# First attention of a fused eight-stage kernel: a searched order of steps, heads' score pieces in turn, a tie step on one tensor, fewer row copies

## What is computed

```python
qkv = layernorm(x) @ w_attn.T + b_attn          # split into q, k, v by head
att = einsum('bhid,bhjd->bhij', q, k) / sqrt(8) # causal
S = relu(att[:, 0]); S[..., 0] = 0; S *= 1 - eye(T)
FF = cumsum(shift_down_one_row(S), axis=1)      # a penalty for each (i, j)
att = att - FF[:, None]
rank = rank of FF within its row (ties: lower j first)
keep = (rank < min(budget - 1, i + 1)) | eye(T) # budget = int(0.2 * 2048) = 409
y = softmax(where(keep, att, -inf)) @ v
x = x + y @ w_proj.T + b_proj
```

## Time and profile before

| | us |
|---|---|
| median of three runs | 2910.46 (2904.49 to 2914.45) |
| the profiled execution | 2907.81 |
| its span in the profile | 2906.0 |
| before the search | 0 to 97 |
| search | 97 to 307 |
| attention | 307 to 926 |
| stages 2 to 8 | 926 to 2906 |
| busy over the span: TensorE, VectorE, ScalarE, GpSimd | 88%, 62%, 62%, 12% |

### The profile page before, as it was taken

One profiled execution on the slowest core, in us unless ns is written; L12 is line 12 of the kernel. 1 busy time (PEld: TensorE's weight loads), 2 busy tenths in 40 slices (PEclk: granted clock), 3 DMA queues, 4 the chain that ended last, 5 costly groups with the idle time before them and its releaser, 6 DMA issues. The chain is left out here.

```text
span 2906.0 us, 73996 instructions
## 1 busy us (share of the span) xinstructions
PE 2553.9 (88%) x30564; PEld 1586.3 (55%) x30564; DVE 1802.5 (62%) x5184; ACT 1796.3 (62%) x3222; POOL 347.1 (12%) x718
## 2 busy tenths in 40 slices
PE   7989788888888999999997999999999999886586
PEld 3668466665665532122113657667667676564355
DVE  6899788777875651000005577787787778653852
ACT  3799565555665269999993266666667667421331
POOL 3100332222220100000000100000000000034025
PEclk8989799999999999999998999999999999897698
DMA  3410001111002011100000000000000000312103
GB/s 118 71 26 2 7 12 17 17 17 17 17 10 55 1 59 54 56 1 1 1 1 17 28 14 8 8 2 7 7 2 8 8 2 2 98 23 40 29 19 55
DMA packets 85111, 68.12 MB, mean 23 GB/s; under 512 B 40776, under 2 KB 73688, under 8 KB 84392
## 3 DMA queue, kind: packets, MB, share of 16 engines
q1 hardware_dynamic: 76328, 57.09, 8.2%
q0 software_dynamic: 8448, 6.30, 1.7%
HBM read 47.21 MB, written 19.96 MB: 23 GB/s over the span
## 5 line engine op out<-in xcount | busy, mean ns | idle before, releaser
L1890 ACT ACTIVATE arena<-ps 128x1024 f32<-128x1024 f32 x512 | 474.1, 1281 | 25.9 <-PE ps L1840 24.0
L1341 DVE CUSTOM_DVE_ANT_0 arena<-ps,arena 128x1024 f32<-128x1024 f32 (+7 forms) x384 | 349.9, 931 | 107.0 <-PE ps L1217 91.1
L2268 DVE CUSTOM_DVE_ANT_0 arena<-ps,arena 128x512 f32<-128x512 f32 (+3 forms) x640 | 371.1, 643 | 26.6 <-PE ps L2132 25.8
L1293 ACT ACTIVATE arena<-ps 128x1024 f32<-128x1024 f32 (+3 forms) x320 | 275.2, 896 | 130.6 <-PE ps L1250 127.0
L2225 ACT ACTIVATE arena<-arena 128x1152 f32<-128x1152 f32 (+15 forms) x256 | 306.4, 1199 | 63.1 <-DVE arena L2268 63.1
L2132 PE MATMUL ps<-arena 64*128 64x512 f32 (+3 forms) x1280 | 270.3, 547 | 3.5 <-ACT arena L2201 1.1
L1851 PE MATMUL ps<-arena 128*32 128x512 f32 x2048 | 273.0, 604 | 0.0
L2163 PE MATMUL ps<-arena 128*64 128x128 f32 x4352 | 262.3, 275 | 0.0
L2163 PEld LDWEIGHTS ps<-arena 128*64 128x64 f32 x4352 | 235.3, 137 | 33.4 <-issue 28.7
L2187 ACT COPY arena<-ps 128x512 f32<-128x512 f32 (+3 forms) x410 | 189.7, 517 | 76.0 <-PE ps L2149 73.7
L1245 PE MATMUL ps<-arena 64*128 64x64 f32 x4352 | 217.0, 232 | 20.4 <-ACT arena L1293 12.2
(11 more groups left out here) (312 smaller groups left out, 4003.9 us busy)
## 6 DMA issues: line engine op xcount, KB each, us to landing
arena<-scr_q SPq DMA_DIRECT2D x256, 32.0 KB
scr_s<-scr_f SPq DMA_DIRECT2D x1, 4096.0 KB, 16.8
arena<-scr_k SPq DMA_DIRECT2D x32, 128.0 KB
arena<-by_head_k SPq DMA_DIRECT2D x16, 192.0 KB
arena<-scr_s SPq DMA_DIRECT2D x16, 192.0 KB, 2.7
arena<-by_head_q SPq DMA_DIRECT2D x28, 96.0 KB
by_head_k<-arena SPq DMA_DIRECT2D x5, 512.0 KB, 4.5
scr_x<-arena SPq DMA_DIRECT2D x2, 1024.0 KB, 5.4
```

What stands on the lines that cost most here:

```text
L1293: e.activation(turned_block(u, kc), src, ACT.Exp, scale=-1.0).then_inc(exped, 1)
L1341: e.tensor_tensor_reduce(scored_block(u, g)[:, lo:hi], PS[:, 1024 * (k % 2):1024 * (k % 2) + hi - lo], NF[t][:, lo:hi], -1.0, mxs[:, col - ...
L1890: e.activation(PTR[k % RS], PS[:, at(n):at(n) + 1024], ACT.Sigmoid, scale=float(1 / np.sqrt(8.0))).then_inc(weighed, 1)
L2268: e.tensor_tensor_reduce(slot(u, t, g)[:, lo:hi], PS[:, base(step) + 512 * g:base(step) + 512 * g + hi - lo], bias, -1.0, mxs[:, col - 1:c ...
```

## The change

- Row copies: q rows of the c-th group of four tiles are copied only to row groups 1 to c, and k rows of chunk c only to row group c: 9 copies instead of 24. They count on the three semaphores `d_q`, one per group, and a matmul waits only for the copies of its own four tiles.
- Pieces: the list of score pieces runs (piece 0 of both heads), (piece 1 of both heads). A second piece waits for its own head's first piece, by number.
- Ties: step 4 was (count > allowed) x (is a tie), reading two tensors; it is now (count > allowed) x -2^-126 by a tensor_scalar that reads the count alone. Step 5 is now (penalty - threshold) > that: at a tie the difference is zero, which is above -2^-126 and not above 0. The two tensors change places in steps 5 and 6.
- Order: `TileOrder` becomes a search. A `Course` is a partial order with its clocks. From each of up to 30 courses every candidate that could start within 0.5 us of the earliest one is tried; of the courses that reach the same counts of steps the one with the least idle time stays (TensorE's idle time counts double), and of all, the 30 with the least. Each instruction has two times: what it takes of its engine and when its result arrives. A change between matmuls of 64 and of 128 rows costs 0.115. GpSimd's split and the blocking by scans are followed; a shift may come at most two units past the last close; a divide is put behind the step that copies its last sums.

Nothing else is changed: the same units, the same instructions per unit, the same banks and extras. The diff, cut to its core:

```diff
+TINY = float(2.0 ** -126)
...
+    def on_tensor(self, rows, ready, lasts, ends):
+        start = self.tensor + (0.115 if self.rows not in (None, rows) else 0.0)
+        if ready > start:
+            self.idle += 2 * (ready - start)
+            start = ready
+        self.rows, self.tensor = rows, start + lasts
+        return start + ends
...
+    BLOCKS = {"turn": ((0.19, 0.34), (0.37, 0.54), (0.55, 0.73), (0.73, 0.91)),
+              "exp": ((0.29, 0.38), (0.5, 0.6), (0.71, 0.81), (0.92, 1.02)),
+              "pv": ((0.11, 0.39), (0.22, 0.4), (0.33, 0.61), (0.44, 0.62))}
...
+        self.pieces = [(u, g, i) for u in range(self.n) for i in range((units[u][0] + 8) // 8) for g in range(2)]
+        self.turns = [(u, kc) for u in range(self.n) for kc in range((units[u][0] + 4) // 4)]
+        self.last = [(t + 4) // 4 - 1 for t, _ in units]
+        self.last_of = {t: u for u, (t, _) in enumerate(units)}
+        courses, best = [Course()], None
+        while courses:
+            reached = {}
+            for c in courses:
+                options = [(max(c.tensor + (0.115 if c.rows not in (None, rows) else 0.0), ready), kind) for kind, rows, ready in self.candidates(c)]
+                if not options and (best is None or c.vector < best.vector):
+                    best = c
+                for start, kind in options:
+                    if start <= min(options)[0] + 0.5:
+                        x = c.copy()
+                        self.go_on(x, kind)
+                        key = (*x.at.values(), len(x.flips), len(x.adds))
+                        if key not in reached or x.idle < reached[key].idle:
+                            reached[key] = x
+            courses = sorted(reached.values(), key=lambda c: c.idle)[:width]
...
-        pieces = [(u, g, i) for u in range(n) for g in range(2) for i in range((units[u][0] + 8) // 8)]
...
-            options = sorted((max(now["pe"] + (0.2 if m != mode[0] else 0.0), ready) + bias.get(kind, 0.0), kind, m) for kind, m, ready in candidates())
...
+    def may_shift(self, c):
+        w = c.at["shift"]
+        if w < min(self.n, c.at["close"] + 3) and (w < 2 or (w - 2, self.last[w - 2]) in c.turned):
+            return self.split_at(c, w)
+        return None
+
+    def candidates(self, c):
+        free = min(c.free) + 0.05
+        if c.at["score"] < len(self.pieces):
+            u, g, i = self.pieces[c.at["score"]]
+            over = self.over(self.scored, u)
+            if u < c.at["shift"] + 4 and (over is None or over in c.turned):
+                yield "score", 64, c.biased[-2] + 0.06 if len(c.biased) >= 2 else 0.0
+        if c.at["turn"] < len(self.turns):
+            u, kc = self.turns[c.at["turn"]]
+            over = self.over(self.turned, u)
+            if u in c.copied and (over is None or over in c.summed):
+                yield "turn", 64, max(c.copied[u] + 0.06, free)
+        v = c.at["close"]
+        kept_back = v >= 1 and self.held(c, v - 1)
+        if v < self.n and (v, self.last[v]) in c.exped and not kept_back:
+            yield "close", 128, max(free, c.exped[v, self.last[v]] - 0.44 * self.last[v] - 0.03)
+        if v == self.n and v - 1 not in c.merged and not kept_back:
+            yield "merge", 128, max(free, c.kept[v - 1] + 0.05)
+        ready = self.may_shift(c)
+        if ready is not None:
+            yield "shift", 128, max(free, ready + 0.06)
+        if c.flips:
+            yield "flip", 128, max(free, c.flips[0][1] + 0.06)
+        if c.adds:
+            yield "add", 128, max(free, c.adds[0][1] + 0.05)
...
+                if x[0] >= 3 and j == 3:
+                    c.scans = c.scans[-2:] + ((c.vector, c.vector + 0.267 * nb),)
...
+        if kind == "close":
+            v = c.at["close"]
+            c.at["close"] += 1
+            use = (s, ("close", v))
+            if v:
+                self.merge(c, v - 1, max(free, c.kept[v - 1] + 0.05), use)
+            w, ready = c.at["shift"], self.may_shift(c)
+            with_shift = ready is not None and ready < c.tensor + 0.2 + 0.055 * (self.units[v][0] + 1)
+            for kc in range(self.last[v] + 1):
+                if with_shift and w not in c.shifted and kc == (self.last[v] + 2) // 2:
+                    self.shift(c, w, ready + 0.06, (None, ("close", v)), 1)
+                end = c.summed[v, kc] = c.on_tensor(128, max(free, c.exped[v, kc] + 0.05), *self.BLOCKS["pv"][self.blocks(v, kc) - 1])
+                c.emit("pv", v, kc, use=use if v == 0 and kc == 0 else None)
...
+        if c.ended and not c.flips and not c.adds and self.last_of[c.ended[0]] in c.taken:
+            t, c.ended = c.ended[0], c.ended[1:]
+            end = c.on_vector(c.taken[self.last_of[t]] + 0.05, 0.49, 0.56)
+            c.emit("divide", t)
+            c.flips += ((t, end),)
+            c.divided += (t,)
...
                 e.dma_start(XB, a["L0_attn_a_b_proj"].unsqueeze(0).to_broadcast([128, 128])).then_inc(d_late, 16)
-                for c in range(4):
-                    for by, ready, of, to in ((filled, 7 + c, q_rows, q_rows), (qkv_biased, 3 * c + 3, k_t, k_rows)):
-                        w.wait_ge(by, ready)
-                        for g in range(1, 4):
-                            e.dma_start(cols(to, c)[32 * g:32 * g + 8, :], cols(of, c)[0:8, :]).then_inc(d_rows, 16)
+                for c in range(1, 4):
+                    w.wait_ge(filled, 7 + c)
+                    for g in range(1, c + 1):
+                        e.dma_start(cols(q_rows, c)[32 * g:32 * g + 8, :], cols(q_rows, c)[0:8, :]).then_inc(d_q[c - 1], 16)
+                    w.wait_ge(qkv_biased, 3 * c + 3)
+                    e.dma_start(cols(k_rows, c)[32 * c:32 * c + 8, :], cols(k_t, c)[0:8, :]).then_inc(d_q[c - 1], 16)
                 rpe_sync(e, w)
                 for i in range(3):
                     w.wait_ge(part, 2 * i + 1)
@@ -740,7 +837,6 @@
 
 
             q_rows, k_rows = reg(D0 + 13312, 2048), reg(D0 + 15360, 2048)
-            d_rows = sem("f_d_rows")
 
             def head_rows(g):
 
@@ -760,7 +856,7 @@
                             w.wait_ge(f_relu, n - 3)
                         g = c0 // 512
                         if g:
-                            w.wait_ge(d_rows, 384)
+                            w.wait_ge(d_q[t // 4 - 1], 16 * (t // 4 + 1))
                         q, k = head_rows(g)
                         e.matmul(bank(n % 4, c1 - c0), q[:, 128 * t:128 * t + 128], k[:, c0:c1], start=True, stop=True).then_inc(f_scores, 1)
                     else:
@@ -1083,7 +1179,7 @@
                 for i, x in enumerate(steps):
                     first = ahead if k == 1 else 0
                     extras.setdefault((16 * (k - 1) + first + (15 - first) * i // len(steps), 1, 0), []).append(x)
-            plan = TileOrder(units, tiles, extras, space, {"score": -0.3, "shift": 0.1, "flip": -0.65, "add": -0.8, "turn": -0.15, "close": -0.3})
+            plan = TileOrder(units, tiles, extras, space, 30)
             fixed, split_p, shifted = sem("a_fixed"), sem("a_split"), sem("a_shifted")
             scores, biased, exped, turned_p = sem("a_scores"), sem("a_biased"), sem("a_exped"), sem("a_turned_p")
             pv_made, merged, copied = sem("a_pv_made"), sem("a_merged"), sem("a_copied")
@@ -1154,11 +1250,11 @@
                 if j == 3:
                     e.tensor_tensor_scan(CS[:, 0:W], E[:, 0:W], E[:, 0:W], 0.0, ALU.add, ALU.max).then_inc(penalty, 1)
                 if j == 4:
-                    e.scalar_tensor_tensor(CS[:, 0:W], CS[:, 0:W], nd, E[:, 0:W], ALU.is_gt, ALU.mult).then_inc(penalty, 1)
+                    e.tensor_scalar(E[:, 0:W], CS[:, 0:W], nd, -TINY, ALU.is_gt, ALU.mult).then_inc(penalty, 1)
                 if j == 5:
-                    e.scalar_tensor_tensor(E[:, 0:W], nf, th, CS[:, 0:W], ALU.is_gt, ALU.max).then_inc(penalty, 1)
+                    e.scalar_tensor_tensor(CS[:, 0:W], nf, th, E[:, 0:W], ALU.subtract, ALU.is_gt).then_inc(penalty, 1)
                 if j == 6:
-                    e.scalar_tensor_tensor(nf, E[:, 0:W], NEG, nf, ALU.mult, ALU.subtract).then_inc(penalty, 1)
+                    e.scalar_tensor_tensor(nf, CS[:, 0:W], NEG, nf, ALU.mult, ALU.subtract).then_inc(penalty, 1)
 
             def attend_sync(e, w):
                 w.wait_ge(f_summed, len(chunks))
@@ -1205,7 +1301,7 @@
                     if kind == "score":
                         g, i = step[2:]
                         w.wait_ge(d_k, 512)
-                        w.wait_ge(d_q[r % 3], 256 * (r // 3 + 1))
+                        w.wait_ge(d_q[r % 3], 16 * (r % 3 + 2) + 256 * (r // 3 + 1))
                         w.wait_ge(counted, len(counts))
                         k, h = plan.no[step], 2 * p + g
                         if k >= 2:
@@ -1327,7 +1423,7 @@
                         lo, hi = 1024 * i, min(1024 * (i + 1), 128 * (t + 1))
                         w.wait_ge(scores, scores_no[step])
                         if i:
```

(62 more changed lines are left out.)

211 lines of the change are left out of this document (117 added, 94 removed).

## The result

| | kernel before | changed kernel |
|---|---|---|
| median of four runs, us | 2910.22 | 2833.77 (2826.20 to 2837.66) |
| ratio of the runs | | 0.9739, 95% interval 0.9718 to 0.9759 |
| span of the profiled run | 2906.0 | 2828.4 |

The change takes off 76.5 us, 2.6%. Forecast were 47 us (2863), so the direction was right, the time lies in the range 2826 to 2904 near its low end, and the size was too small by 29 us. The measured time lies nearer to rival C (2823) than to the forecast itself.

What follows compares the result with a forecast made beforehand. In-order TensorE and VectorE, neither full, wait for each other in the attention. Start 5, six pairs 35, first pair 3, last pair and tail 4 sum to 47 us: 2860.8 from the profiled run, 2863 on the median; range 2826 to 2904.

Steps and rivals of the forecast that it cites:

- rival C: Both engines pack tightly in the attention: 67 us a pair, 8 at the start, 6 and 8 at the ends; 2823, chance 0.12.
- Part 1: Start of the kernel: fewer row copies remove TensorE's 4.10 us stall and a little low clock; 5 us, bounds 0 and 12.
- Part 2: Penalty's tie step in the attention: 1549 to 546 ns, 13.0 us less on VectorE, counting only as far as VectorE is late.
- Part 3: Score pieces of tiles 8 to 15: 0.23 us saved on each of 91 second pieces, 20.9 us of VectorE, no new wait.
- rival E: Attention's score pieces: the skill's rule holds, so heads in turn is worth nothing; 2875, chance 0.04.
- Part 4: Attention's order by search: six pairs from 77.8 to 72 us each, 35 us; first pair 3, last pair and tail 4.
- the floor: Six middle pairs: TensorE's 66.1 us busy at the last pair's 93% gives 71.1 us a pair; 72 taken.
- B: Six middle pairs: TensorE, the busier engine, takes all relief as waits; only 2 us gained each; 2893, chance 0.18.
- D: Attention slower: sums ahead of unready exponentials double TensorE's 61.0 us weight-load waits for ScalarE; 2924, chance 0.07.
- F: Tie step in the attention does not get faster: 2 us a pair back on VectorE; 2871, chance 0.03.

## Why the prediction was right, and short by more than a third

**Part 1, copies: right.** 5 us forecast, 6.2 measured alone (interval 2 to 9); the stall of 4.10 us is gone.

**Part 2, tie step: the duration right, its weight wrong.** Forecast 546 ns at the mean width, measured 549 mean and 7.1 us in all, 13.0 less. I said that it counts only as far as VectorE is late and put all the first pair's gain at 3 us. The tie step alone made 6.3 us there, from 2.4 us of work: the large penalties of tiles 7 and 15 lie beside small tiles. I had not counted that the step holds up GpSimd's splits, nor that the low clock of that pair could move.

**Part 3, heads in turn: the 0.23 us right, "no cost" wrong under the old order.** The gaps went as forecast. VectorE's need was forecast at 60.5 us a pair and is busy 60.63. I wrote that the short pieces of tiles 8 to 10 cost nothing; alone, the last pair lost 6.9 us, and the whole gained at most 5. With everything but the search the last pair is just as long (98.4). With the search the loss is 1.2. Whether it comes from the banks' turns or from the greedy planner's preferences on the new list isn't settled.

The Trainium skill's rule ("VectorE: DVE Perf Modes", "The DRAIN you can't avoid") would have had the taking back of this part make no difference (rival E). The trace disagrees: the start at 578.47 comes with the read, where the 89 second pieces before start 0.14 to 0.15 us after its end. So for this pair of instructions a wait on the one just ahead costs 0.23 us that the same pair without it doesn't. What the 0.23 us are worth in the whole is less sure: the 10.3 us of the taking back come with a new plan.

**Part 4, the term that was mis-sized.** The 35 us for the six pairs were to be the search and VectorE's relief together. The runs separate them:

| six pairs, us | old tie and heads | new tie and heads |
|---|---|---|
| old order | 466.9 | 451.5 |
| searched order | 430.4 | 405.2 |

The search by itself gives 36.5, my number for both. The relief gives 15.4 under the old order and 25.2 under the searched one, and the search 46.3 on top of the relief. That each makes the other worth more is likely but not shown: the two mixed cases come from profiled executions 8 to 9 us above their medians, by the medians themselves the two together bring only 7 us more than their sum (76.9 against 48.4 and 21.2), and the searched order with the old tie was planned for a tie step that it does not have. The step that failed is the floor, "66.1 / 0.93 = 71.1" and 72 taken. Both of its inputs were off. TensorE went to 95%, not 92. And its busy time was not a fixed amount of work: it fell from 66.1 to 64.1 us a pair. By the clock records the six pairs spent 34.1 us at 1.2 GHz before and 6.8 after. Half of the difference is 13.6 us, and the busy time of the six fell by 12.2 (396.8 to 384.6). The second profile of the changed kernel has 10.2 us and 386.3. I had seen the granted clock of 0.94 to 0.98 and not counted it. With fewer waits of TensorE there are fewer falls of the clock; the last section has what stood before one. That the waits cause them is argued, no run isolates it.

**Sum.** 26.7 us too little in the six pairs and 5.1 in the first; the rest came out within 3 us each.

**Rivals.** C (67 us a pair, 2823) is what happened in the pairs, at 67.5, and is nearer to the measured 2834 than my 2863; the range holds it, the sum behind the forecast does not reach it. I gave it 0.12 because it "asks for 98% of TensorE", which rested on the same fixed 66.1. B is refuted by its own test, VectorE's waits fell from 67.0 to 37.0. D did not happen, TensorE's weight loads wait less for exponentials than before (48.4 against 61.0), but a slower end was real: an order searched on wrong times costs 87 us (one time per step). It went by late scores, not by late exponentials as I had it. E is refuted by the starts in the trace, F by the 549 ns.

## What to carry to other kernels

When two engines are each late for the other, first find out how much of their waiting is order. Here the order alone brought 48 of 77 us, and the relief for VectorE 15 us of some 34 under the old order (21.2 with the copies' 6.2). By one profile each, the 10.6 us that the tie step takes off VectorE in the six pairs gave 0.9 us under the old order and 7.1 under the new one; the medians point the same way but aren't clear of noise. So test small savings again after the order is repaired, and look at more than the engine that they are taken from: the tie step also freed GpSimd. A planner's search needs true times. Told too much work for TensorE it did harm (87 us), without the blocked neighbours it lost 10 us, and with one course instead of 30 it lost 62. A busy share taken as a floor should first be freed of its time at the low clock.

## What the runs showed of the hardware

TensorE's busy time is no fixed amount of work. Less half of the time at 1.2 GHz, the six pairs come to 379.7 us in the kernel before and 377.3 with the old order and the rest new; both change 259 times between matmul groups of 64 and of 128 rows (counted in the traces, over the attention). The changed kernel has 355 changes and 381.2 us, the search alone and the changed kernel with the pieces head by head have 377 and 388.6 and 389.3, the single course 389 and 390.2. So orders that change groups more often went with more TensorE busy time, by up to 10 us; the searched order pays this and still wins. The changes can't be the whole cause: the kernel with one time per step has 359 of them, about as many as the changed kernel, and 402.3 us.

The granted clock fell where TensorE had been waiting. In the kernel before it was 0.50 from 458.3 to 461.7 us; in the stretch ahead of that TensorE was busy 4.04 of 6.80 us, where its mean in the six pairs is 85%:

```profile
451.50:458.30 6.80, 4.04 (x91) 2.51 (x80) 4.53 (x11) 2.60 (x8) 0.22 (x2) 1.00 0.01 3
```

Ahead of four more such falls it was busy 3.90 to 5.36 us of as long a stretch. Whether waiting of this size always brings the clock down was not looked at.

GpSimd stands still under more than scans. In the kernel before, the first step of a split, 0.19 to 0.20 us long beside the score pieces, lasted to the end of the VectorE instruction that it started under when that was a scan (4.26 us under 4.42), a scalar_tensor_tensor (2.25 under 2.35) or the tensor_scalar from fp32 to bf16 (1.18 under 1.28); the counting step L1149 did not hold it up. The planner of the change knows only of the scans.

The stretch before the search varied between profiled runs of the same code: 92.8, 97.0 and 90.9 us in three kernels with nine copies. The 4.2 us of the first table could not have been read from one profile; the timed rounds (6.2 us) carry it, and so does the mean of all profiles: 93.3 us in ten with nine copies, 98.2 in four with 24.
